# Readouts beside a recurrence: a new order on POOL, ACT and DVE, the last sum folded into ACT, and no ballast products in six bodies

## The chip, the cores and the metric
One core of a Trainium2 chip. The metric is the device time of one execution in microseconds; the time given for a kernel is the median of its runs.

## The reference, cut to what matters
Input x is (8, 512, 64, 2), output (8, 512, 128). Three layers follow each other: a token layer `h` (four small attentions), a recurrent layer whose output is added to h, and a last layer that adds the layernorm of h to h (what else it adds is addressed to channels from 128 on, of which there are none).

```
x_norm = ln(layernorm(h)) ;  xin = x_norm @ W_in.T
res_step: new = tanh(xin_t + prev @ W_res.T);  new = 0.95 * new + 0.05 * prev      # 512 steps
ssm_step: s = A_bar_t * prev + B_bar_t                                             # 512 steps
readout(s) = gelu(ln(s) @ W_ro.T + b_ro)
gate = sigmoid(layernorm(h) @ W_gate.T + b_gate)
h = h + readout(res) * gate + readout(ssm) * (1 - gate)
out = h + layernorm(h)                                                             # rstd*h - rstd*mean + h
```

## The kernel before
Work is cut into 32 tiles, each one batch row and a quarter (128 positions) of the sequence: h_all and gate_all hold them as [128 positions, tile, 128 channels]. The recurrence has 512 steps in 32 bodies of 16. All engines run programs written out in one order, coupled by semaphores alone; an instruction that waits holds all behind it on its engine. The order is written by hand: each engine loops over bodies i and steps t, does its part of the step first (`scan`), and then what is placed beside that step.

A step goes round three engines. PE adds W_res times the state to a PSUM region in four groups of small products (L1150 with y16 as high and low weights, L1157, L1150 with y_lo, L1162). ACT reads that with three operations: tanh to fp16 (L535, y16), tanh to fp32 (L536, ys), the carry (L538, kp16). DVE makes the rests y_lo (L838: ys - y16, both in SBUF) and kp_lo (L841). PE needs y_lo and kp_lo before the step is done.

Bodies 0 to 23 have the attention tiles beside the steps, 24 and 25 the set-up of the second recurrence (ssm). In the last six, 26 to 31, three things stand beside the steps:
- `feed(s, c)`, 8 per body (at even t): PE multiplies B (L1284); DVE first runs the ssm scan of the feed before (`recur`, L953, increments ssm_done), then waits for PE's product and makes the next scan's input (L944). PE's feed s waits for ssm_done of the scan s-2: its PSUM bank is then free.
- `sigma`, DVE scans that turn the tanh values into states (L889): a full row of 128 at t = 1 and 5, and in bodies 28 to 31 a half row of 64 at t = 3, 7, 11, 15.
- `readout(u, n, ...)`, with u = t % 4 and n the group number: every group of four steps starts one readout tile, and five tiles are under way at once. In group n the functions work on tiles n (reads), n-1 (statistics, r_dev, L1005), n-2 (gelu, blend), n-3 (layernorm statistics, norm) and n-4 (last sum).

A tile's way through the readout: PE reads (L1299, four products: (0,0) in u=1, (0,1) in u=2, (1,0) in u=3, (1,1) in the next u=0; ballast products of 512 columns, `keep_clock`, L1074, ahead of the first and third). DVE takes statistics of both reads (L991, L998). POOL makes r_var and r_dev (L454, L458). DVE scales the reads out of PSUM (L1005, readout_scaled). ACT does gelu (L581). POOL blends: difference, base, product, sum into h_all (L436, L437, L465, L471). DVE takes the statistics for the layernorm (L982, L987). POOL makes -mean, var + eps, rstd and -mean*rstd (L443 to L449, ln_small). ACT scales and shifts h_all into gate_all (L574, `norm`), POOL adds h_all to that (L429), and SP's queue writes the tile out on r_out (L350). ACT also halves and shifts the gate (L593).

Reads of tile n go to two PSUM banks that tile n-2 had. PE therefore waits, ahead of the first read:

```
pe.wait_ge(readout_scaled, n - (3 if alone else 1) + TWO_FREE)      # TWO_FREE: counts that are there from the start
```

After the last step `rest_of_readouts` runs the remaining 12 groups with nothing beside them (`alone=True`); there DVE does the blend (L961 to L969).

## Time and profile before

| | |
|---|---|
| time, median of 3 runs | 720.89 us (720.78 to 721.06) |
| the profiled execution: its time, its span | 724.85 us, 723.1 us |
| busy: PE, DVE, ACT, POOL | 654.3 (90%), 567.7 (79%), 424.3 (59%), 193.9 (27%) us |
| last chain by engine | PE 65%, DVE 14%, POOL 9%, issue 7%, ACT 4% |
| POOL busy, tenths, last 10 of 40 slices | 3 8 7 8 7 8 7 7 7 6 |
| granted PE clock, the same slices | 9 9 9 9 9 9 9 9 9 7 |

The shares are of the whole span; the change touches the last 164 us, from about 559 us on, where POOL is busy for 7 to 8 tenths. A clock digit of 9 stands for 90% of full speed or more. The recurrence ends at 680.5 us, the 12 groups without steps after that.

### The profile page before, as it was taken

Reading aid. Unit: us, or ns where it says so; the run is one execution under the profiler, and the core shown is the slowest. Engines: PE = TensorE matmul, PEld = TensorE weight load, DVE = VectorE, ACT = ScalarE, POOL = GpSimd, SP = SyncE. Lnnn points to the kernel's source line nnn. Section 1 sums busy time; section 2 is a strip of 40 time slices with the busy share of each in tenths; the row PEclk is TensorE's granted clock in tenths of the full one; section 3 lists DMA queues with packets and bytes.
Section 4 is the critical chain, followed back from the end, with each engine's and each line's share of the span. In section 5 each row is a group of like instructions: output and inputs, shape, how many; then the busy total and the mean of one; then the engine's idle time right before and its main releaser. Section 6 shows DMA issues by size and latency. Waiting matters only on the chain.

```text
span 723.1 us, 28488 instructions
## 1 busy us (share of the span) xinstructions
PE 654.3 (90%) x11161; PEld 500.4 (69%) x11161; DVE 567.7 (79%) x2438; ACT 424.3 (59%) x2051; POOL 193.9 (27%) x429
## 2 busy tenths in 40 slices
PE   6777777789999999999999999999999999999772
PEld 2334444447888888888888888888787777777641
DVE  4685454567888888989899899899647788988885
ACT  3455544447766776677767776677464444444432
POOL 1133333331000100000000000000000387878776
PEclk9677788899999999999999999999999999999997
DMA  5000000000000000000000000000000000000000
GB/s 185 1 0 1 2 1 1 1 2 3 4 3 4 4 3 5 3 3 4 3 4 3 4 3 4 4 3 5 2 3 2 2 17 14 13 18 13 13 19 26
DMA packets 6326, 7.27 MB, mean 10 GB/s; under 512 B 688, under 2 KB 4784, under 8 KB 6192
## 3 DMA queue, kind: packets, MB, share of 16 engines
q1 hardware_dynamic: 5904, 4.46, 2.0%
q8 instruction: 88, 1.44, 0.9%
q10 hardware_dynamic: 288, 0.99, 0.4%
q14 instruction: 46, 0.38, 0.2%
HBM read 3.35 MB, written 2.10 MB: 8 GB/s over the span
## 4 chain that ended last, share of the span: by engine, by line
PE 65%; DVE 14%; POOL 9%; issue 7%; ACT 4%; DMA 1%; POOLq 0%; DVEq 0%; ACTq 0%
PE PS L1150 22%; PE PS L1202 13%; PE PS L1074 4%; PE PS L1162 4%; PE PS L1117 3%; PE PS L1168 2%; PE PS L1118 2%; POOL r_dev L458 2%; PE PS L1127 2%; PE PS L1051 2%; POOL ln_small L446 2%; PE PS L1104 2%; PE PS L1087 2%; PE PS L1157 2%; DVE top L761 1%
## 5 line engine op out<-in xcount | busy, mean ns | idle before, releaser
L535 ACT ACTIVATE y<-PS 128x16 f16<-128x16 f32 x512 | 94.3, 184 | 167.9 <-PE PS L1162 165.6
L1202 PE MATMUL PS<-ballast,ident 128*128 128x220 f16 (+5 forms) x722 | 150.9, 284 | 0.0
L1150 PE MATMUL PS<-y_lo,res_hi 128*128 128x8 f16 x2048 | 128.7, 169 | 8.8 <-DVE y_lo L838 7.2
L838 DVE TENSOR_TENSOR y_lo<-ys,y 128x16 f16<-128x16 f32 x512 | 95.4, 186 | 51.3 <-ACT ys L536 47.3
L1150 PEld LDWEIGHTS PS<-y,res_hi 128*128 128x128 f16 x2048 | 96.6, 96 | 55.6 <-ACT y L535 21.4
L1150 PE MATMUL PS<-y,res_hi 128*128 128x8 f16 x2048 | 128.8, 169 | 0.4 <-ACT y L535 0.3
L1150 PE MATMUL PS<-y,res_lo 128*128 128x8 f16 x2048 | 123.4, 166 | 0.0
L841 DVE SCALAR_TENSOR_TENSOR kp_lo<-PS,setup,kp 128x16 f16<-128x16 f32 x512 | 114.8, 224 | 0.0
L401 POOL TENSOR_TENSOR small<-small,minus_half 128x2 f32<-128x2 f32 x32 | 22.7, 709 | 340.9 <-DVE y_lo L838 280.1
L517 ACT ACTIVATE prob<-PS,exp_up,sc 128x512 f32<-128x512 f32 x128 | 101.0, 789 | 17.8 <-PE PS L1104 17.8
L761 DVE TENSOR_REDUCE top<-PS 128x1 f32<-128x512 f32 x128 | 86.8, 681 | 21.4 <-PE PS L1087 21.4
L1074 PE MATMUL PS<-ballast,ident 128*128 128x512 f16 (+1 forms) x275 | 89.2, 401 | 15.6 <-DVE ys L889 9.6
L522 ACT ACTIVATE prob_hi<-PS,exp_up,sc 128x512 f16<-128x512 f32 x128 | 100.8, 788 | 0.0
L536 ACT ACTIVATE ys<-PS 128x16 f32<-128x16 f32 x512 | 99.0, 193 | 0.0
L1150 PEld LDWEIGHTS PS<-y_lo,res_hi 128*128 128x128 f16 x2048 | 85.4, 96 | 18.1 <-DVE y_lo L838 13.2
L538 ACT ACTIVATE kp<-PS 128x16 f16<-128x16 f32 x512 | 97.3, 190 | 0.0
L1162 PE MATMUL PS<-kp_lo,carry_id 128*128 128x16 f16 x512 | 92.2, 180 | 0.0
L1150 PEld LDWEIGHTS PS<-y,res_lo 128*128 128x128 f16 x2048 | 87.5, 96 | 0.0
L1157 PE MATMUL PS<-kp,carry_id 128*128 128x16 f16 x512 | 86.5, 169 | 0.0
L791 DVE TENSOR_TENSOR prob_lo<-prob,prob_hi 128x512 f16<-128x512 f32 x96 | 65.4, 682 | 0.0
L1117 PE MATMUL PS<-keep,prob_hi 128*128 128x66 f16 x512 | 51.0, 198 | 6.3 <-ACT prob_hi L522 6.2
L1202 PEld LDWEIGHTS PS<-ballast,ident 128*128 128x128 f16 x722 | 56.5, 97 | 0.2
(205 smaller groups left out, 1337.7 us busy)
## 6 DMA issues: line engine op xcount, KB each, us to landing
ys<-in_x SPq DMA_DIRECT2D x8, 256.0 KB, 7.5
out<-gate_all SPq DMA_DIRECT2D x32, 64.0 KB, 1.5
mats<-in_mats ACTq DMA_DIRECT2D x1, 709.0 KB, 5.3
rows<-in_rows ACTq DMA_DIRECT2D x1, 257.5 KB, 7.5
wall<-in_wall SPq DMA_DIRECT2D x1, 256.0 KB, 5.0
```

The source lines that it names most:

```text
L517: a_.activation(prob[:, a, :], X[a], ACT.Exp, scale=e_col[:, j % B:j % B + 1], bias=exp_up[:, :])
L522: a_.activation(prob_hi[:, a, :], X[a], ACT.Exp, scale=e_col[:, j % B:j % B + 1], bias=exp_up[:, :]).then_inc(prob_ready, 1)
L535: a_.activation(y16[:, :].rearrange("p (m b) -> p m b", m=NH), pre, ACT.Tanh, scale=back).then_inc(y16_ready, 1)
L536: a_.activation(ys[:, :, bass.ds(i * STEPS + (1 + t), 1)].rearrange("p (m b) o -> p m (b o)", m=NH), pre, ACT.Tanh, scale=back).then_inc(a ...
L538: a_.activation(kp16[:, :].rearrange("p (m b) -> p m b", m=NH), pre, ACT.Copy, scale=keep_scale).then_inc(kp_ready, 1)
L838: v.tensor_tensor(y_lo[:, :], ys[:, :, bass.ds(i * STEPS + (1 + t), 1)].rearrange("p n o -> p (n o)"), y16[:, :], ALU.subtract).then_inc(l ...
L841: v.scalar_tensor_tensor(kp_lo[:, :].rearrange("p (m b) -> p m b", m=NH), PRE[t % 2][:, r, :, t // 2, :], setup[:, 24:25], kp16[:, :].rear ...
L1074: t_.matmul(bank[:, 0:size], ident16[:, :], ballast[:, 0:size], start=True, stop=True, skip_group_check=True)
L1150: t_.matmul(dst[:, m, :], wts[:, k, m * P:m * P + P], st[:, k * B:k * B + B], start=False, stop=False, skip_group_check=True)
L1157: t_.matmul(dst, carry_id[:, :], kp16[:, :].rearrange("p (m b) -> p m b", m=NH), start=False, stop=False, skip_group_check=True)
L1162: t_.matmul(dst, carry_id[:, :], kp_lo[:, :].rearrange("p (m b) -> p m b", m=NH), start=False, stop=True, skip_group_check=True).then_inc( ...
L1202: t_.matmul(at[:, 0:size], ident16[:, :], ballast[:, 0:size], start=False, stop=True, skip_group_check=True)
```

## The change
On POOL, in the groups beside steps: the layernorm's small operations (now a function `last_norm`, for tile n-4) move from u=2 to u=0, the four blend operations stand together in u=2, and r_var/r_dev move from u=2 to u=3. The sum L429 is gone: `last_norm` adds one operation, rstd + 1, and ACT's norm computes (1 + rstd) * h - mean * rstd in one pass and releases the output itself. On ACT, gelu moves from u=0 to u=1, and norm, still in u=3, works on tile n-4. On DVE, the scaling of the reads (now `scale_reads`) moves from u=3 to the next u=0, the layernorm statistics from u=0 and 1 to u=1 and 2, the half scans from u=3 to u=0, and the feeds, on PE too, from u = 0 and 2 to u = 2 and 3. The ballast products ahead of reads remain only in the groups without steps. PE's waits are unchanged.

```diff
@@ POOL @@
             def readout(u, n, e, active, fed, kept_bodies, alone=False):
-                if 4 in active and u == (3 if alone else 0):
-                    j = n - 4
-                    pool.wait_ge(readout_normed, j + 1 + TWO_FREE)
-                    pool.sem_inc(pool_waited, 1)
-                    res = gate_all[:, bass.ds(j, 1), :].rearrange("p o n -> p (o n)")
-                    g.tensor_tensor(res, res, h_all[:, bass.ds(j, 1), :].rearrange("p o n -> p (o n)"), ALU.add
-                                    ).then_inc(r_out, 1)
-                if 2 in active and u == 1 and not alone:
+                def last_norm(j, s):
+                    pool.wait_ge(ln_stats, j + 1 + FREE)
+                    if j > 1:
+                        pool.wait_ge(r_out, j - 1)
+                    g.tensor_tensor(ln_small[:, s, 2:3], ln_mv[:, s, 0:1], minus_one[:, :], ALU.mult)
+                    g.tensor_tensor(ln_small[:, s, 0:1], ln_mv[:, s, 1:2], eps_col[:, :], ALU.add).then_inc(ln_var_ready, 1)
+                    pool.wait_ge(ln_var_ready, j + 1)
+                    g.tensor_tensor(ln_small[:, s, 1:2], ln_small[:, s, 0:1], minus_half[:, :], ALU.pow
+                                    ).then_inc(ln_pow_ready, 1)
+                    pool.wait_ge(ln_pow_ready, j + 1)
+                    g.tensor_tensor(ln_small[:, s, 0:1], ln_small[:, s, 1:2], ones[:, 0:1], ALU.add)
+                    g.tensor_tensor(ln_small[:, s, 2:3], ln_small[:, s, 2:3], ln_small[:, s, 1:2], ALU.mult
+                                    ).then_inc(ln_dev_ready, 1)
+
+                if 4 in active and u == 0 and n <= IN_SCAN:
+                    last_norm(n - 4, e)
+                if 2 in active and u == 2 and not alone:
                     j = n - 2
                     now = h_all[:, bass.ds(j, 1), :].rearrange("p o n -> p (o n)")
                     pool.wait_ge(r_gelu, j + 1 + TWO_FREE)
                     pool.wait_ge(h2_ready, j + TWO_FREE)
                     g.tensor_tensor(r_diff, r_act[:, e, 0, :], r_act[:, e, 1, :], ALU.subtract).then_inc(r_diff_ready, 1)
                     g.tensor_tensor(r_base, r_act[:, e, 1, :], now, ALU.add).then_inc(r_base_ready, 1)
-                if 3 in active and u == (3 if alone else 2):
-                    j = n - 3
-                    s = 1 - e
-                    pool.wait_ge(ln_stats, j + 1 + FREE)
-                    pool.wait_ge(readout_normed, j - 1 + TWO_FREE)
-                    g.tensor_tensor(ln_small[:, s, 2:3], ln_mv[:, s, 0:1], minus_one[:, :], ALU.mult)
-                    g.tensor_tensor(ln_small[:, s, 0:1], ln_mv[:, s, 1:2], eps_col[:, :], ALU.add).then_inc(ln_var_ready, 1)
-                    pool.wait_ge(ln_var_ready, j + 1)
-                    g.tensor_tensor(ln_small[:, s, 1:2], ln_small[:, s, 0:1], minus_half[:, :], ALU.pow
-                                    ).then_inc(ln_pow_ready, 1)
-                    pool.wait_ge(ln_pow_ready, j + 1)
-                    g.tensor_tensor(ln_small[:, s, 2:3], ln_small[:, s, 2:3], ln_small[:, s, 1:2], ALU.mult
-                                    ).then_inc(ln_dev_ready, 1)
-                if 1 in active and u == 2:
-                    ...
+                if 1 in active and u == (2 if alone else 3):
+                    j = n - 1
+                    pool.wait_ge(r_stats, j + 1)
+                    g.tensor_tensor(r_var[:, :], r_mv[:, :, 1:2].rearrange("p r o -> p (r o)"), r_eps[:, :], ALU.add
+                                    ).then_inc(r_var_ready, 1)
+                    pool.wait_ge(r_var_ready, j + 1)
+                    pool.wait_ge(readout_scaled, j - 1 + TWO_FREE)
+                    g.tensor_tensor(r_dev[:, 1 - e, :], r_var[:, :], minus_half[:, :].to_broadcast([P, 2]), ALU.pow
+                                    ).then_inc(r_dev_ready, 1)
+                if 3 in active and u == 3 and alone:
+                    last_norm(n - 3, 1 - e)
@@ ACT @@
-                                  scale=ln_small[:, s, 1:2], bias=ln_small[:, s, 2:3]).then_inc(readout_normed, 1)
+                                  scale=ln_small[:, s, 0:1], bias=ln_small[:, s, 2:3]).then_inc(r_out, 1)
-                if 2 in active and u == 0 and not alone:
+                if 2 in active and u == 1:
                     gelu(n - 2)
-                if 2 in active and u == 1 and alone:
-                    gelu(n - 2)
-                if 3 in active and u == 3 and not alone:
-                    norm(n - 3, 1 - e)
-                if 4 in active and u == 2 and alone and n > IN_SCAN:
+                if 4 in active and u == (2 if alone else 3):
                     norm(n - 4, e)
@@ DVE @@
-                if i >= BODIES - NQ and t in (3, 7, 11, 15):
+                if i >= BODIES - NQ and t % 4 == 0:
                     n = (i - (BODIES - NQ)) * 4 + t // 4
                     sigma_row(n % NH, NT - B + n // NH, 0, P // 2, sigma_half)
+            def scale_reads(j, e):
+                dve.wait_ge(r_dev_ready, j + 1 + FREE)
+                dve.wait_ge(r_gelu, j - 1 + TWO_FREE)
+                for r in range(2):
+                    last = v.scalar_tensor_tensor(r_pre[:, e, r, :], PS[:, read_banks(j, e) + r, H:H + P],
+                                                  r_dev[:, e, r:r + 1], ro_row[:, :], ALU.mult, ALU.add)
+                last.then_inc(readout_scaled, 1)
...
-                if 3 in active and u == (2 if alone else 0):
+                if 3 in active and u == (2 if alone else 1):
...
-                if 3 in active and u == (2 if alone else 1):
+                if 3 in active and u == 2:
...
-                if 1 in active and u == 3:
-                    ...
+                if 1 in active and u == 3 and alone:
+                    scale_reads(n - 1, 1 - e)
+                if 2 in active and u == 0 and n <= IN_SCAN:
+                    scale_reads(n - 2, e)
...
-                    if t % 2 == 0:
-                        feed(t // 2, i - FIRST_DECAY)
+                    if t % 4 > 1:
+                        feed(t // 4 * 2 + t % 2, i - FIRST_DECAY)
                     body_readouts(readout, t, i)
@@ PE @@
                         pe.wait_ge(readout_scaled, n - (3 if alone else 1) + TWO_FREE)
-                    keep_clock(PS[:, read_banks(n, e), :])
+                    if alone:
+                        keep_clock(PS[:, read_banks(n, e), :])
                     read_one(0, 0, n, e)
                 if 0 in active and u == 2:
                     read_one(0, 1, n, e)
                 if 0 in active and u == 3:
                     pe.wait_ge(ssm_done, fed + EIGHT_FREE)
-                    keep_clock(PS[:, read_banks(n, e) + 1, :])
+                    if alone:
+                        keep_clock(PS[:, read_banks(n, e) + 1, :])
                     read_one(1, 0, n, e)
...
-                    if t % 2 == 0:
-                        feed(t // 2, i - FIRST_DECAY)
+                    if t % 4 > 1:
+                        feed(t // 4 * 2 + t % 2, i - FIRST_DECAY)
                     body_readouts(readout, t, i)
```

## Rows read from the trace of the kernel before

**Rows 1.** L535 in bodies 27 and 28 to 31: count, min/median/max ns, first and last start.
```profile
L535 ACT ACTIVATE y<-PS x16: 184/184/185, 577.1 to 597.0; 128x16 f16<-128x16 f32 x16
...
L535 ACT ACTIVATE y<-PS x64: 184/184/185, 598.5 to 680.5; 128x16 f16<-128x16 f32 x64
```

**Rows 2.** Timeline, one group with a full scan: start, us, engine, line, out<-in [idle before].
```profile
603.42 0.47 PE L1284 MATMUL PS<-xn,b_t 128*128 128x128 f32 x2
603.60 0.18 ACT L535 ACTIVATE y<-PS 128x16 f16<-128x16 f32 x1 [0.28 <-PE PS L1162]
...
604.14 0.61 DVE L1005 SCALAR_TENSOR_TENSOR k<-PS,r_dev,ro_row 128x128 f32<-128x128 f32 x2 [0.62 <-POOL r_dev L458]
604.16 0.24 PE L1150 MATMUL PS<-y,res_hi 128*128 128x8 f16 x4
...
604.79 0.42 ACT L581 ACTIVATE k<-k 128x256 f32<-128x256 f32 x1 [0.85 <-DVE k L1005]
...
605.69 0.45 POOL L436 TENSOR_TENSOR k<-k 128x128 f32<-128x128 f32 x1
...
605.78 0.39 DVE L838 TENSOR_TENSOR y_lo<-ys,y 128x16 f16<-128x16 f32 x1
...
606.24 0.59 DVE L889 TENSOR_TENSOR_SCAN ys<-keep_row,ys 128x128 f32<-128x128 f32 x1
...
606.59 0.18 ACT L535 ACTIVATE y<-PS 128x16 f16<-128x16 f32 x1 [1.00 <-PE PS L1162]
...
607.48 0.16 DVE L838 TENSOR_TENSOR y_lo<-ys,y 128x16 f16<-128x16 f32 x1
...
607.70 0.47 DVE L953 TENSOR_TENSOR_SCAN keep<-keep 128x128 f32<-128x128 f32 x1
...
608.05 0.18 ACT L535 ACTIVATE y<-PS 128x16 f16<-128x16 f32 x1 [0.83 <-PE PS L1162]
...
608.43 0.14 DVE L838 TENSOR_TENSOR y_lo<-ys,y 128x16 f16<-128x16 f32 x1
...
608.51 0.24 PE L1150 MATMUL PS<-y,res_hi 128*128 128x8 f16 x4
...
608.63 0.34 DVE L889 TENSOR_TENSOR_SCAN ys<-keep_row,ys 128x64 f32<-128x64 f32 x1
...
609.05 0.18 ACT L535 ACTIVATE y<-PS 128x16 f16<-128x16 f32 x1 [0.29 <-PE PS L1162]
```

**Rows 3.** Timeline, the group before: y_lo and POOL starting together.
```profile
600.37 0.45 POOL L437 TENSOR_TENSOR k<-k,h_all 128x128 f32<-128x128 f32 x1
600.37 0.48 DVE L838 TENSOR_TENSOR y_lo<-ys,y 128x16 f16<-128x16 f32 x1 [0.24 <-ACT ys L536]
```

**Rows 4.** Timeline of POOL, a group without a full scan, from r_dev to r_dev.
```profile
634.63 0.70 POOL L458 TENSOR_TENSOR r_dev<-r_var,minus_half 128x2 f32<-128x2 f32 x1
...
635.96 0.46 POOL L471 TENSOR_TENSOR h_all<-k 128x128 f32<-128x128 f32 x1 [0.20 <-POOL k L465]
636.38 0.57 POOL L429 TENSOR_TENSOR gate_all<-gate_all,h_all 128x128 f32<-128x128 f32 x1
636.91 0.45 POOL L436 TENSOR_TENSOR k<-k 128x128 f32<-128x128 f32 x1
...
637.73 0.19 POOL L443 TENSOR_TENSOR ln_small<-ln_mv,minus_one 128x1 f32<-128x1 f32 x1
...
639.59 0.70 POOL L458 TENSOR_TENSOR r_dev<-r_var,minus_half 128x2 f32<-128x2 f32 x1
```

**Rows 5.** Timeline, the end of the kernel: POOL on the last two tiles.
```profile
717.42 0.19 POOL L449 TENSOR_TENSOR ln_small<-ln_small 128x1 f32<-128x1 f32 x1
...
718.73 0.19 POOL L443 TENSOR_TENSOR ln_small<-ln_mv,minus_one 128x1 f32<-128x1 f32 x1
...
720.67 0.45 POOL L429 TENSOR_TENSOR gate_all<-gate_all,h_all 128x128 f32<-128x128 f32 x1 [0.70 <-ACT gate_all L574]
```

**Rows 6.** Busy time by engine in a stretch; after POOL the granted clock, DMA share, GB/s.
```profile
510.00:514.00 4.00, 4.00 (x81) 3.13 (x79) 1.47 (x10) 1.29 (x12) 0.00 (x0) 0.58 0.02 4
```

More of the change, by code:

```diff
@@ L284, in build @@
         ln_dev_ready = sem("ln_dev_ready")
-        readout_normed = sem("readout_normed")
         stats_waited = sem("stats_waited")
@@ L293, in build @@
         start_free = (r_dev_ready, ln_stats)
-        start_two_free = (ln_dev_ready, readout_normed, readout_scaled, r_gelu, h2_ready)
+        start_two_free = (ln_dev_ready, readout_scaled, r_gelu, h2_ready)
         def tile_q(j):
@@ L999, in readout @@
                     last.then_inc(r_stats, 1)
-                if 1 in active and u == 3:
-                    j = n - 1
-                    dve.wait_ge(r_dev_ready, j + 1 + FREE)
-                    dve.wait_ge(r_gelu, j - 1 + TWO_FREE)
-                    for r in range(2):
-                        last = v.scalar_tensor_tensor(r_pre[:, 1 - e, r, :], PS[:, read_banks(n - 1, 1 - e) + r, H:H + P],
-                                                      r_dev[:, 1 - e, r:r + 1], ro_row[:, :], ALU.mult, ALU.add)
-                    last.then_inc(readout_scaled, 1)
+                if 1 in active and u == 3 and alone:
+                    scale_reads(n - 1, 1 - e)
+                if 2 in active and u == 0 and n <= IN_SCAN:
+                    scale_reads(n - 2, e)
             dve.wait_ge(pv_done, NA * NT)
```

8 lines of the change are left out of this document (removed).

## The prediction

> **What bounds the kernel now.** First I read the starts of L535, the tanh with which every step of the recurrence begins on ACT, body by body: body 27 has its first and last start at 577.1 and 597.0, bodies 28 to 31 (64 steps) run from 598.5 to 680.5 [rows 1]. With the step after each, body 27 takes 21.4 us (577.1 to 598.5) and each of the last four about 20.8 (82.0 x 64/63 / 4), 5.2 per group of four steps (u = 0 to 3), in which one readout tile goes through.
>
> Then the timeline of one group of body 28 [rows 2]. The reader is to see two things. A step that is not held up takes 1.00 (608.05 to 609.05). The others are: the group takes 5.45. In u=0 DVE's L1005 waits 0.62 for POOL's r_dev, and the step's y_lo stands behind it; in u=1 y_lo (L838) takes 0.39 instead of 0.14, because POOL's L436 is reading SBUF (605.69 to 606.14); in u=2 it is late behind a full-width scan and the statistics (606.24 to 607.48). Third, POOL's own queue in a group without a full scan [rows 4]: from r_dev to r_dev 4.96, There POOL is the bound, as far as these rows follow each other without a gap (L471, L429, L436); where a full scan is due (t=1 and 5, half of the groups), DVE's queue adds to it. PE is never the one that is late for long.
>
> **What goes.** (a) L429, POOL's last sum: 0.53 to the next start (636.38 to 636.91) [rows 4], against one more 128x1 operation at 0.14 (its neighbours are 0.19 long and overlap). POOL's queue then takes 4.96 - 0.53 + 0.14 = 4.57, or less where it waits for DVE within that: a bound of at most 4.6. (b) The readout chain is spread out: r_dev is computed in u=3, used by L1005 in the next u=0, gelu in u=1, the blend on POOL in u=2. The 0.62 stall of y_lo goes. (c) 48 ballast products (2 in each of 24 groups). In u=3 a step with ballast and a read still took 1.00, so that one was hidden; in u=1 DVE was late anyway. I cost them at 0; if nothing had hidden them, at their own length, under 0.4 each, 18 us in all would be the other end, which the 1.00 step excludes.
>
> **What is late next.** I walk through a group of bodies 28 to 31, with y0 = 0 the start of its first tanh, from [rows 2, 3]. y_lo comes at +0.38 (608.43 - 608.05), other DVE work starts at +0.58 (608.63). That is now the half scan, 0.34 long, some 0.26 to the next start, since DVE's operations overlap by 0.08 (estimate); then L1005, 0.61, done at 1.45. Two waits that stand unchanged in the code now bite, because what they wait for was moved:
>
> (d) PE's first read of the tile in u=1 waits for readout_scaled of the tile two before, whose banks it takes. That was done in the last group before; now it is L1005 in this very group. PE has to stand with the read at the head of its queue, and the next step's matmuls behind it, until 1.49. From a read's start to the next tanh it is 0.43 + 0.54 = 0.97: feed and read hold the next step's matmuls back by 0.74 (603.42 to 604.16), of which I give the feed 0.31 and the read 0.43 by their columns (estimate), and from those matmuls to the tanh it is 0.54 (608.51 to 609.05). So y2 = 2.46. Without (d) it would be 2.0; now it is 2.99 (603.60 to 606.59), so the first two steps still win 0.5.
>
> (e) PE's feed in u=3 waits for ssm_done of the feed two before, which DVE makes in the feed just before it. These were two steps apart; in u=2 and u=3 they are one apart. DVE's scan L953 is 0.47 long [rows 2] and starts 0.58 after y2, so PE can feed at y2 + 1.10. With 0.74 and 0.54 behind it y4 = y2 + 2.38, where steps of 1.09 and 1.00 pass in groups without a full scan. This loses 0.2.
>
> (f) The four 128x128 operations of POOL, 0.45 each, now stand in u=2. gelu (0.42) starts after L1005 at 1.49, so POOL begins at 1.98, the product at 2.80, the sum at 3.46 (two in 0.82, and [0.20] of waiting before the sum, [rows 4]). y_lo of u=2 comes at 2.46 + 0.38 = 2.84: it meets the product. [Rows 3] show what that costs: L838, started together with L437, ended when that did, 0.48 against 0.14. So y_lo is some 0.4 late, and with it L953, PE's feed and y4: 2.46 + 2.38 + 0.4 = 5.2. If it slips in ahead of the product, 4.85. With a full scan, DVE reaches y_lo at 1.58 + 0.4 + 0.2 + 0.65 = 2.85 by itself (1.24 from 606.24 to 607.48 is a slowed scan plus the 0.65 of L991), the same place, so 5.2 as well. Full-scan groups take 5.4 now, the others 5.0.
>
> In [rows 2] L838 that came during L436 ended within 0.03 of its end, while the scan L889, which met L437 for 0.3, took 0.59, only 0.12 more than L953, a scan of the same size. The Trainium skill, page "SBUF — State Buffer", section "Who interferes with whom", says that a DVE instruction with two SBUF inputs and a GpSimd instruction that reads SBUF share one interface, and that whichever starts first blocks the other entirely. The row of L838 agrees, that of the scan only in part. By that rule the moved blend speaks against the change: y_lo loses up to 0.45 in u=2, and the group is 5.2 to 5.3; by the scan's row it would be 4.95.
>
> **The sum.** Bodies 28 to 31: 16 groups; 8 with a full scan save 0.2 each (5.4 to 5.2), 8 without lose 0 to 0.2; together -0.5, with ends -6 (4.85 in all groups) and +5 (5.5). Body 27 has no half scan: L1005 is done at 1.19, y2 = 2.20, gelu starts at 1.34 behind ACT's own three operations; y_lo at 2.58 comes while POOL's second operation runs (2.24 to 2.69), 0.15 lost; its groups take 4.6 and, with a full scan, 5.0: 19.2, so -2.2 (ends -4 and 0). Body 26: its first two groups, without a readout to wait for, lose 0.2 each by (e), the other two win that; 0. The end of the kernel [rows 5]: the last norm on POOL started at 718.73 behind the sum of the tile before; now it can at 717.42 + 0.14 + 0.20 = 717.76, and ends 0.14 later; the last sum after the last norm, 0.70 waited and 0.45 long, of which 0.50 is the ACT operation itself, goes with 0.65: -0.97 + 0.14 - 0.65 = -1.5. The first tile after the recurrence: reads start once DVE is through its queue, which has the same operations in another order; -0.3 (ends -0.5 and +0.3). Other tiles of this stage are bound by DVE's unchanged queue: 0. Sum: -0.5 - 2.2 - 1.5 - 0.3 = -4.5, on the profiled execution 724.85 to 720.3. The median of the runs, 720.89, lies 3.96 below that execution, and I take the same difference: 716.4.
>
> **The rivals.**
> 1. The clash with POOL is missed: y_lo gets in ahead of the product, groups of 4.6 to 4.85. For it: the margin is a few hundredths, in [rows 2] y_lo got in at the end of L436 although L437 was due, and POOL may shift. Against it: [rows 3]. 16 groups x 0.35 to 0.6 = 5.6 to 9.6 instead of 0.5: 707 to 711.5, say 710.
> 2. Nothing is left but the end: the last four bodies come out a little longer than now, as the two waits on PE and the port give back more than was won; the time is 720.
> 3. Slower: wait (e) compounds with (f). y_lo of u=2 loses 0.45, the scan L953 behind it meets POOL's sum and takes 0.12 more, and y_lo of u=3 meets that sum too, 0.15. The group is then 2.46 + 2.38 + 0.45 + 0.12 + 0.15 = 5.55, 16 x 0.35 = 5.6 lost, 4.0 won elsewhere, of which 1 goes in body 27: 723.5. It decides from a group of 5.2 + 4.0/16 = 5.45. For it: all these operations are back to back in u=2 and u=3. Against it: the sum ends at 3.92, and y_lo of u=3 isn't due before 4.1.
> 4. The clock falls without ballast. The granted clock was 0.58 from 510 to 514 though PE was busy the whole of it [rows 6], so a busy PE is no guarantee. Against it: reads and feeds stay, and the group is no longer. At the half clock PE's reads and feeds, about 2.2 of a group, double: from 2 or 3 such groups on the gain is gone, over the whole stage it would be 40 us.
>
> **How the numbers follow.** Forecast 0.43 (716.4; 713.5 to 719); rival 1 0.25; rival 2 0.16; rival 3 0.12; rival 4 0.04. About 0.2% (1.4 us) can be told from no change: faster 0.43 + 0.25 + 0.06 of rival 2 = 0.74; within 0.2% the other 0.10 of rival 2 and 0.01 of rival 3 = 0.11; slower 0.11 + 0.04 = 0.15. The range 708.5 to 722.5 leaves out the far part of rival 1, the top of rival 3 and rival 4.
>
> **What would show it.** L1005 without a wait for r_dev in the scan stage; the tanh to tanh time of u=1 at 1.3 to 1.5 with PE waiting for L1005; PE's feed in u=3 waiting for L953; L838 of u=2 at 0.4 or more beside POOL's L465; in the last lines no POOL operation after the last norm. It is wrong if POOL's r_dev still ends the wait of u=0, if the half scan isn't what delays the read in u=1 (bodies 26 and 27 should be faster than the later ones), or if the granted clock shows dips between 560 and 680.

## The result and the profile after

The kernel got slower. Its median is 737.28 us (729.05 to 738.45, 4 runs) against 720.91 us for the kernel before, run beside it: a ratio of 1.0196, 95% interval 1.0147 to 1.0244. The prediction was 716.4 (708.5 to 722.5). The profiled execution took 737.34 us with a span of 735.5 us; before it was 724.85 and 723.1. In the later sets three single executions of the kernel before, at 746.46, 747.73 and 923.14 us, lie far off all the others and are left out of the ratios.

The page of after, first the busy times by engine, then the granted PE clock in tenths over 40 slices of 18.4 us:

```profile
PE 666.2 (91%) x11113; PEld 508.2 (69%) x11113; DVE 565.1 (77%) x2438; ACT 422.9 (57%) x2051; POOL 188.6 (26%) x429
...
PEclk9788888899999999999999999999996557599998
```

PE has 48 products fewer (11113 against 11161) and is busy 11.9 us longer. The weight loads beside it (PEld) grew too, 508.2 against 500.4; DVE, ACT and POOL did not. The clock line says why: where the line of before has 9, five slices from about 552 us on have 6, 5, 5, 7, 5. They lie in the stretch from which the ballast was taken out; the last slices of that stretch are back at 9.

The busy times by stretch (stretch in us; its length; busy us and instructions of PE, PEld, DVE, ACT, POOL; granted clock as a share of 2.4 GHz; DMA share; GB/s) show it closer:

```profile
556.00:560.00 4.00, 3.27 (x50) 2.82 (x51) 2.15 (x12) 1.81 (x13) 0.00 (x0) 0.88 0.01 2
560.00:602.00 42.00, 42.00 (x441) 32.49 (x440) 26.21 (x124) 12.74 (x89) 20.13 (x52) 0.50 0.02 6
602.00:608.00 6.00, 6.00 (x68) 5.12 (x65) 3.38 (x16) 2.21 (x15) 4.12 (x11) 0.60 0.04 11
608.00:614.00 6.00, 5.50 (x87) 4.45 (x85) 5.22 (x26) 2.40 (x17) 3.62 (x9) 1.00 0.05 14
614.00:620.00 6.00, 5.18 (x64) 4.10 (x65) 4.83 (x24) 2.42 (x15) 4.62 (x14) 0.75 0.05 14
620.00:641.00 21.00, 20.54 (x217) 15.95 (x214) 13.88 (x66) 6.92 (x45) 12.00 (x33) 0.50 0.04 11
641.00:695.00 54.00, 45.64 (x724) 37.73 (x721) 46.48 (x224) 25.64 (x161) 42.37 (x114) 1.00 0.05 15
```

For 42 us from 560 on the clock is at 0.50, the lower of its two levels (1.2 GHz), with PE busy for all 42.00 of them. It is back between 608 and 614, lost again until 641, and then stays at 1.00 to the end of the recurrence. PE runs 10.5 products per us in the second row and 13.4 in the last. So within this kernel a high busy share of PE is the sign of the low clock: each product lasts longer. One line's products, the reads out of `keep` between 577 and 602 and between 650 and 694 (median and longest in ns stand in the middle and at the end of the three numbers), last longer at the low clock:

```profile
L1295 PE MATMUL PS<-ro_pair,keep x16: 634/634/774, 579.7 to 601.2; 128*128 128x256 f32 x16
L1295 PE MATMUL PS<-ro_pair,keep x34: 379/380/463, 650.1 to 691.3; 128*128 128x256 f32 x34
```

The medians are 634 and 380 ns: x1.67, not 2, for half the clock.

A group at the low clock, in order of time (start, duration, engine, line and operation, in brackets the idle time before it and what ended it). L531 is the tanh with which a step begins, L1280 the feed, L1295 the read:

```profile
590.40 0.78 PE L1280 MATMUL PS<-xn,b_t 128*128 128x128 f32 x2
590.58 0.18 ACT L531 ACTIVATE y<-PS 128x16 f16<-128x16 f32 x1 [0.83 <-PE PS L1158]
...
590.96 1.06 PE L1295 MATMUL PS<-ro_pair,ys 128*128 128x256 f32 x2
...
592.42 0.18 ACT L531 ACTIVATE y<-PS 128x16 f16<-128x16 f32 x1 [1.22 <-PE PS L1158]
...
594.26 0.18 ACT L531 ACTIVATE y<-PS 128x16 f16<-128x16 f32 x1 [1.13 <-PE PS L1158]
...
595.67 0.18 ACT L531 ACTIVATE y<-PS 128x16 f16<-128x16 f32 x1 [1.08 <-PE PS L1158]
```

No PE line has a wait in brackets: PE goes from product to product, and everything else waits for it. Steps with feed and read take 1.84 (590.58 to 592.42 to 594.26), the one with a read alone 1.41 (594.26 to 595.67); with the fourth step, 1.47, the group is 6.6.

The same at the full clock, bodies later:

```profile
675.80 0.18 ACT L531 ACTIVATE y<-PS 128x16 f16<-128x16 f32 x1 [0.73 <-PE PS L1158]
676.61 0.58 DVE L967 SCALAR_TENSOR_TENSOR k<-PS,r_dev,ro_row 128x128 f32<-128x128 f32 x2
676.71 0.18 ACT L531 ACTIVATE y<-PS 128x16 f16<-128x16 f32 x1 [0.57 <-PE PS L1158]
...
677.34 0.67 PE L1295 MATMUL PS<-ro_pair,ys 128*128 128x256 f32 x2 [0.66 <-DVE k L967]
...
678.38 0.18 ACT L531 ACTIVATE y<-PS 128x16 f16<-128x16 f32 x1 [0.74 <-PE PS L1158]
678.55 0.46 POOL L451 TENSOR_TENSOR k<-k,gate_all 128x128 f32<-128x128 f32 x1
678.69 0.35 DVE L830 TENSOR_TENSOR y_lo<-ys,y 128x16 f16<-128x16 f32 x1
679.10 0.47 DVE L945 TENSOR_TENSOR_SCAN keep<-keep 128x128 f32<-128x128 f32 x1
679.47 0.18 ACT L531 ACTIVATE y<-PS 128x16 f16<-128x16 f32 x1 [0.47 <-PE PS L1158]
679.62 0.49 PE L1280 MATMUL PS<-xn,b_t 128*128 128x128 f32 x2 [0.18 <-DVE keep L945]
...
680.92 0.18 ACT L531 ACTIVATE y<-PS 128x16 f16<-128x16 f32 x1 [0.73 <-PE PS L1158]
```

Steps 0.91, 1.67, 1.09, 1.45: the group is 5.12 where it was 5.45 [rows 2]. So the change does what it is for, once the clock is there. L967, which answers to L1005, waits for nothing; the waits that the prediction called (d) and (e) are both there in brackets, 0.66 and 0.18.

Body by body, from first tanh to first tanh, bodies 26 to 31 (the last without its last step):

```
before  17.97  21.38  20.58  20.80  20.81  19.81    sum 121.35
after   24.64  26.63  24.72  22.87  20.45  19.02    sum 138.33
```

The sum grows by 17.0 us. What follows the last tanh takes 1.9 less (735.5 - 694.8 = 40.7 against 723.1 - 680.5 = 42.6), and this execution reached body 26 2.7 us earlier, before any changed instruction (its early stretch had no dip such as [rows 6] has). 17.0 - 1.9 - 2.7 = 12.4, the difference of the spans. Without the 2.7, which the change did not bring, it is 15.1, near the 16.4 of the medians.

Where the clock first fell, at about 559: the last thing ahead of it is a load of ACT's function table at the end of body 25, and with it the widest stop of PE thereabouts.

```profile
555.19 1.28 ACT L599 ACT_TABLE_LOAD   x1
...
556.73 0.26 PE L1146 MATMUL PS<-y,res_hi 128*128 128x8 f16 x4 [0.83 <-ACT y L531]
```

The kernel before has the same load (557.88, 1.28 us) and keeps its clock; there a feed stands in the stop, and PE waits 0.32 instead of 0.83.

Where it rose, at about 607 and 641, PE was running the input products of the step regions (L1164), a short stretch of extra work, or had just done so:

```profile
605.36 1.20 PE L1164 MATMUL PS<-xd,in_t 128*128 128x128 f32 x4
...
639.10 0.77 PE L1164 MATMUL PS<-xd,in_t 128*128 128x128 f32 x2
```

### The profile page after: what moved, and what is told of

Its sections match the earlier page's. It is cut to its first block, busy times and chain, and to the rows that moved or that the text cites. A ratio compares the mean times of both kernels' runs of the same rounds, so it can differ in the third digit from the quotient of the medians.

```text
span 735.5 us, 28357 instructions
## 1 busy us (share of the span) xinstructions
PE 666.2 (91%) x11113; PEld 508.2 (69%) x11113; DVE 565.1 (77%) x2438; ACT 422.9 (57%) x2051; POOL 188.6 (26%) x429
## 3 DMA queue, kind: packets, MB, share of 16 engines
q8 instruction: 87, 1.43, 0.8%
## 4 chain that ended last, share of the span: by engine, by line
PE 75%; DVE 14%; issue 5%; ACT 4%; POOL 1%; DMA 1%; DVEq 0%; POOLq 0%; ACTq 0%
PE PS L1146 24%; PE PS L1198 13%; PE PS L1295 7%; PE PS L1070 4%; PE PS L1158 4%; PE PS L1280 3%; PE PS L1164 3%; PE PS L1113 2%; PE PS L1114 2%; PE PS L1123 2%; PE PS L1153 2%; DVE k L967 2%; PE PS L1100 2%; PE PS L1083 2%; PE PS L1047 1%
## 5 line engine op out<-in xcount | busy, mean ns | idle before, releaser
L531 ACT ACTIVATE y<-PS 128x16 f16<-128x16 f32 x512 | 94.3, 184 | 201.0 <-PE PS L1158 199.9
L830 DVE TENSOR_TENSOR y_lo<-ys,y 128x16 f16<-128x16 f32 x512 | 94.3, 184 | 84.4 <-ACT ys L532 79.9
L1146 PEld LDWEIGHTS PS<-y,res_hi 128*128 128x128 f16 x2048 | 100.9, 99 | 65.1 <-ACT y L531 21.8
L1146 PE MATMUL PS<-y,res_hi 128*128 128x8 f16 x2048 | 130.9, 170 | 0.9 <-ACT y L531 0.8
L1070 PE MATMUL PS<-ballast,ident 128*128 128x512 f16 (+1 forms) x227 | 71.2, 406 | 14.7 <-DVE ys L881 8.8
```

Of the source, the lines that this page charges most:

```text
L531: a_.activation(y16[:, :].rearrange("p (m b) -> p m b", m=NH), pre, ACT.Tanh, scale=back).then_inc(y16_ready, 1)
L830: v.tensor_tensor(y_lo[:, :], ys[:, :, bass.ds(i * STEPS + (1 + t), 1)].rearrange("p n o -> p (n o)"), y16[:, :], ALU.subtract).then_inc(l ...
L1070: t_.matmul(bank[:, 0:size], ident16[:, :], ballast[:, 0:size], start=True, stop=True, skip_group_check=True)
L1146: t_.matmul(dst[:, m, :], wts[:, k, m * P:m * P + P], st[:, k * B:k * B + B], start=False, stop=False, skip_group_check=True)
```

## The experiments

The theory after the result: the whole loss is the clock, and the ballast products are what kept it. The rivals: the new order itself is slower (its waits on PE, the clash with POOL), and the low clock is only a mark beside that; or the new order, by its gaps, is what drops the clock, and the ballast has no part. Later runs ask where in the group ballast has to stand, and what the order is worth by itself. All kernels ran with the kernel before beside them; its medians were 723.45, 723.26, 723.98 and 723.31 in the four sets, so ratios are what compares. Each kernel has one traced execution, and what is said of its groups and its clock is of that one.

### Ballast back in the new order

```diff
-                    if alone:
-                        keep_clock(PS[:, read_banks(n, e), :])
+                    keep_clock(PS[:, read_banks(n, e), :])
...
-                    if alone:
-                        keep_clock(PS[:, read_banks(n, e) + 1, :])
+                    keep_clock(PS[:, read_banks(n, e) + 1, :])
```

> The kernel after with the two ballast products of each group back in the six bodies, and nothing else. Theory A (the granted clock is the loss: the kernel after ran about 12 groups of its six bodies at the half clock, 6.57 a group against 5.12 at the full one): the clock stays at 1.00 from 560 to the end of the recurrence. The ballast isn't free in the new order, since PE is what is late there: 0.22 more in u=1, behind the wait for L1005, and 0.22 in u=3, behind the wait for the feed, so groups of 5.5 and a time near 724, between before (720.9) and after (737.3). Theory B (the waits that the new order puts on PE let the clock fall, with ballast or without): half clock in these bodies again, 733 or more.

Measured: 724.01 (722.04 to 726.54, 10 runs), 1.0017 [0.9998, 1.0035]. By stretch:

```profile
555.00:568.00 13.00, 12.05 (x173) 9.63 (x172) 8.01 (x37) 4.88 (x32) 0.00 (x0) 0.87 0.02 4
568.00:685.00 117.00, 103.80 (x1572) 86.00 (x1570) 95.14 (x468) 51.62 (x329) 87.51 (x232) 1.00 0.05 13
```

The clock falls at the same place, about 560, but comes back after some 3.4 us (0.87 over 13 us), and then holds 1.00 for 117 us. That gives back nearly all of the loss: 1.96% slower becomes no difference that can be told. The order is not what makes it slow. But it is not faster than before either: groups take 5.32 (0.91, 1.81, 1.09, 1.52) and not 5.12, 0.14 of it in u=1 and 0.07 in u=3, because in u=1 the ballast now starts only when PE's wait for L967 is over, ahead of the read, on the path:

```profile
650.01 0.58 DVE L967 SCALAR_TENSOR_TENSOR k<-PS,r_dev,ro_row 128x128 f32<-128x128 f32 x2
...
650.74 0.38 PE L1070 MATMUL PS<-ballast,ident 128*128 128x512 f16 x1 [0.67 <-DVE k L967]
...
650.96 0.59 PE L1295 MATMUL PS<-ro_pair,ys 128*128 128x256 f32 x2
```

PE stood idle 0.67, and then did ballast: 0.22 from its start to the read's.

### The old order without ballast

The kernel before, with the two `if alone:` of the change and nothing else of it.

```diff
-                    keep_clock(PS[:, read_banks(n, e), :])
+                    if alone:
+                        keep_clock(PS[:, read_banks(n, e), :])
```

> The kernel before without the ballast products of the reads beside steps, its order unchanged. Theory A (ballast holds the clock in any order): the granted clock falls in these bodies and the time is 728 or more. Theory B (it is the new order that lets it fall): the clock holds as before, groups stay at 4.96 and 5.45, 720 to 721.

Measured: 748.1 (747.19 to 750.22, 4 runs), 1.0344 [1.0325, 1.0364]. By stretch:

```profile
560.00:602.00 42.00, 42.00 (x443) 32.48 (x443) 27.60 (x125) 13.29 (x94) 20.20 (x52) 0.50 0.02 7
602.00:644.00 42.00, 41.33 (x440) 32.87 (x440) 31.50 (x138) 14.90 (x96) 26.86 (x71) 0.58 0.05 13
644.00:686.00 42.00, 39.95 (x489) 31.80 (x488) 33.69 (x151) 16.67 (x105) 29.57 (x77) 0.70 0.05 13
686.00:708.00 22.00, 22.00 (x235) 17.24 (x233) 17.06 (x73) 7.91 (x53) 14.33 (x39) 0.50 0.04 10
```

The second rival falls: the old order loses the clock in the same place, and stays without it longer. Removing the ballast costs 25 us in the old order (748.1 - 723.45) and 13 in the new one (737.28 - 724.01, over two sets). In the traces the old order was low for longer, since it lost the clock three times (at about 560, 618 and 669) and the new one twice; one execution of each doesn't show that the order is the reason.

### Ballast in the first body only

```diff
-                    if alone:
+                    if alone or n < 4:
```

> The kernel after with ballast in body 26 alone (the first four groups), where the clock fell. Theory A1 (the sparse first groups are what lets it fall, later ones hold a full clock): 1.00 throughout, groups of 5.12, 714 to 717. Theory A2 (the groups without ballast can't hold it in general; it fell a second time at 614 to 620 in the run of after): half clock somewhere in bodies 27 to 31, 725 or more.

Measured: 723.9, 727.19, 735.42 and 728.75, median 727.97, 1.0104 [1.0048, 1.0161]. The profiled one is the fastest, and its clock row

```profile
568.00:681.00 113.00, 97.67 (x1535) 81.03 (x1534) 96.42 (x467) 52.02 (x331) 86.67 (x232) 1.00 0.05 13
```

shows 113 us at 1.00 with no ballast in five of the six bodies, and PE busy for 86% only. Theory A1 is wrong in its first part, since the clock fell at 561 even with this ballast and was back at 568. At the full clock the groups without ballast can hold it. But the other three executions took 3 to 12 us more, as theory A2 has it, and where they lost it is not known, since they have no trace.

### Ballast in the first three steps of body 26 only

```diff
+                    if i == FIRST_READ and t < 3:
+                        for _ in range(3):
+                            keep_clock(PS[:, 3, :])
```

> The kernel after with nine ballast products in the first three steps of body 26 and none later. There PE stood idle behind ACT's table load and the clock fell. Theory C (the loss is one fall at a sparse place, from which groups without ballast don't come back): with the place filled the clock stays at 1.00 in most executions, 717 to 720. Theory D (the groups without ballast let it fall by themselves): falls further on, 725 or more in most executions, a wide spread.

Measured: 726.23 (723.71 to 733.04, 10 runs), 1.0050 [1.0023, 1.0076].

```profile
560.00:577.00 17.00, 15.76 (x242) 12.77 (x239) 12.25 (x59) 6.26 (x47) 5.24 (x11) 1.00 0.01 2
577.00:608.00 31.00, 29.77 (x356) 23.98 (x355) 21.45 (x104) 11.26 (x74) 19.86 (x54) 0.67 0.04 10
```

With nine products beside the first steps the fall at 560 is gone from the trace. The profiled execution, the slowest of the ten (span 731.3), then lost the clock at about 585, in body 27, had it back at 606 behind the input products, and lost it again from 619 to 636. So the fall at 560 is not the only one: without ballast it can fall at other places. That is theory D: 7 of the 10 executions took over 725 us, and none came to the 717 to 720 of theory C. Against the change with its clock kept (0.9960, below) the median is 0.9% longer, where it was 2.4% without any ballast, so more than half of the loss goes with the fall at 560.

### Feeds apart again, with ballast

```diff
-                    if t % 4 > 1:
-                        feed(t // 4 * 2 + t % 2, i - FIRST_DECAY)
+                    if t % 2 == 0:
+                        feed(t // 2, i - FIRST_DECAY)
```

> The kernel after with ballast back and with the feeds at u=0 and 2 again (and one more wait of DVE on its own count ahead of the first row after the recurrence, which its order needs). Theory (the wait of PE's feed on the scan of the feed just before is worth 0.2 to 0.3 a group): against the kernel after with ballast alone, u=3 shrinks from about 1.66 to 1.0, but L1005 comes a feed (0.57) later in u=0 and with it the read in u=1, so groups of 5.3 to 5.5, 0 to 3 us faster than it, 721 to 724. Rival (feeds' place does not matter, the port clash of y_lo does): the same time within 1 us.

The two ballast products are back here, and DVE has the one more wait that the expectation names.

Measured: 723.66 (720.91 to 725.34, 10 runs), 1.0007 [0.9992, 1.0022]; groups 5.38 (1.09, 2.20, 1.09, 1.00). The wait (e) is gone, u=3 falls from 1.52 to 1.00, and what it gave is paid in u=0 (1.09 for 0.91, it has a feed now) and u=1 (2.20 for 1.81): DVE's scan L945 and L936 now stand ahead of L967, which ends later, and the ballast and the read wait for it. Undoing this part neither gains nor loses.

### Half scan behind the scaling, with ballast

```diff
-                if i >= BODIES - NQ and t % 4 == 0:
...
+                    half_sigma(t, i)                   # the same scan, behind body_readouts
```

> The kernel after with ballast back, and the half scan of bodies 28 to 31 behind the scaling of the reads (L967) in u=0 instead of ahead of it. Theory (PE's first read of a tile waits for L967, which the half scan holds up by 0.26): u=1 shrinks from 1.81 to 1.57 as in body 27, groups from 5.32 to 5.1, 3 to 4 us less than with ballast back alone (724.0), near 720.5. Rival (DVE's whole queue is the bound, so its order doesn't matter): the same time, and the 0.26 shows up in u=1 or u=2 again.

Measured: 723.4 (719.55 to 725.12, 10 runs), 1.0007 [0.9988, 1.0026]. In the trace u=1 falls from 1.81 to 1.57 and the groups from 5.32 to 5.22 and 5.08, so the half scan does delay L967, as (d) has it; 16 groups by 0.1 to 0.24 are 1.6 to 3.8 us, and less than the runs scatter. What (d) says is shown by the trace; that it is worth time is not shown by the times.

### Ballast where PE waits anyway

```diff
                 if 0 in active and u == 1:
+                    if not alone:
+                        pe.wait_ge(ssm_scaled, ...)
+                        for _ in range(1):
+                            keep_clock(PS[:, 7, :])
...
+                    if t % 4 == 3:
+                        keep_clock(PS[:, read_banks(0, t // 4 % 2) + 1, :])
```

> The kernel after with the same two ballast products a group, but where PE stands idle: in u=1 ahead of the wait for L967 (into a feed bank that is free by then), in u=3 ahead of the feed's wait (into the bank of the next read). Theory (the kernel after lost by the clock alone, and its waits leave room for ballast): groups of 5.12 at the full clock, no half clock from body 27 on, about 4 us less than with ballast back in its old places: 718 to 720, faster than before by 3 to 5. Rival (ballast costs its length wherever it is, or does not hold the clock there): 723 or more.

Measured: 720.99 (718.26 to 722.64, 10 runs), 0.9965 [0.9949, 0.9981]. The product in u=1 stands now ahead of the wait for L967, in bank 7, a feed's bank that is free by then, the other ahead of the feed's wait in u=3. Groups are 5.12 and, in body 27, 4.92, as with no ballast, at

```profile
568.00:679.00 111.00, 104.19 (x1555) 80.08 (x1553) 95.09 (x459) 51.29 (x324) 86.60 (x232) 1.00 0.05 14
```

Against the first experiment the stretch of the six bodies is 4.9 us shorter in the traces (120.6 against 125.5, 24 groups by 0.2), and what follows the last tanh 1.1 longer (40.8 against 39.7), perhaps because DVE is further behind by then, which was not looked into. That leaves 3.8 us, and the ratios, 1.0017 and 0.9965, say 3.8 as well.

### One ballast product a group

The same with the product in u=1 alone.

> The kernel after with one ballast product a group, in u=1 ahead of the wait for L967, none in u=3. Theory (what lets the clock fall is how little PE streams in a group, in degrees): between the kernel after (737) and the one with two idle products (721.0), in an execution either held or not: 721 to 730, with a wide spread of its runs. Rival (only the idle stretch ahead of L967 matters, not the amount): as with two, 721.

Measured: 720.83 (719.91 to 721.93, 7 runs), 0.9960 [0.9948, 0.9972]; groups 5.12.

```profile
568.00:677.00 109.00, 98.40 (x1501) 77.98 (x1498) 93.79 (x454) 50.85 (x321) 85.42 (x229) 1.00 0.05 14
```

One product of 0.38 us in a group, beside a wait, makes the difference between 737.28 (1.0196) and 720.83 (0.9960), 2.4%. The theory of degrees gets no support: the time is that of two products, as the rival has it, and the runs lie close together. This is the nearest to what the prediction had in mind: the change in full, at the full clock but for 559 to 562.5.

### Ballast in the gaps and the half scan last

> Ballast in the idle places, two products in u=1, and the half scan behind L967. Both theories together: groups of 4.9 in bodies 27 to 31, full clock, 714 to 717. If the second ballast product in u=1 no longer fits ahead of L967 (0.4 of idle for 0.43 of products), 0.1 more a group.

Measured: 717.39 (715.72 to 719.31, 4 runs), 0.9922 [0.9891, 0.9952], groups 5.01 and 4.87. (It has two products in u=1 and one in u=3.) Against the kernel with one product in each place (720.99, same set) it is 3.6 us faster. In the traces 2.4 of that lie in bodies 28 to 31 (78.2 against 80.6), where the half scan's place tells, and 1.2 in body 26 (18.86 against 20.08), which here kept its clock at 560. So the half scan's place, which hid in the scatter above, is worth some 2.4 us.

### The folded sum alone

The kernel before, with nothing of the change but `last_norm`'s extra operation and ACT's one pass instead of POOL's L429.

```diff
                     g.tensor_tensor(ln_small[:, s, 0:1], ln_small[:, s, 1:2], ones[:, 0:1], ALU.add)
...
-                                  scale=ln_small[:, s, 1:2], bias=ln_small[:, s, 2:3]).then_inc(readout_normed, 1)
+                                  scale=ln_small[:, s, 0:1], bias=ln_small[:, s, 2:3]).then_inc(r_out, 1)
```

> The kernel before, its order, its ballast, with the last sum folded into ACT's norm and nothing else. Theory (POOL's queue is the bound of the groups without a full scan, and the end is a chain over POOL): groups of 4.96 become 4.6, those of 5.45 stay as they are (their POOL waits for DVE), and the end is 1.5 shorter: 3 to 5 us less than before. Rival (DVE's and PE's queue take over at once): only the 1.5 of the end.

Measured: 717.23 (716.91 to 719.3, 4 runs), 0.9930 [0.9904, 0.9956]. POOL from r_dev to r_dev:

```profile
670.18 0.70 POOL L452 TENSOR_TENSOR r_dev<-r_var,minus_half 128x2 f32<-128x2 f32 x1
...
674.92 0.70 POOL L452 TENSOR_TENSOR r_dev<-r_var,minus_half 128x2 f32<-128x2 f32 x1
```

4.74 where [rows 4] have 4.96. This one part, with order and ballast left as they were, brings 0.70%; in the traces it is 4.5 us in the six bodies (116.9 against 121.35) and 1.5 behind them (41.0). Most groups run at 4.75 to 5.15. Nothing else of the change is needed for it.

### Feeds in u=1 and u=3, half scan last, ballast in the gaps

```diff
-                    if t % 4 > 1:
-                        feed(t // 4 * 2 + t % 2, i - FIRST_DECAY)
+                    if t % 2 == 1:
+                        feed(t // 2, i - FIRST_DECAY)
...
-                if 3 in active and u == (2 if alone else 1):     # layernorm statistics, one step later
+                if 3 in active and u == 2:
...
                 if 0 in active and u == 1:
+                    if not alone:
+                        pe.wait_ge(ssm_scaled, ...)
+                        keep_clock(PS[:, 7, :])
...
                 if 0 in active and u == 2:
+                    if not alone:
+                        keep_clock(PS[:, read_banks(n, e) + 1, :])
```

> The new order with PE's feeds at u=1 and 3, so that the first stands in PE's idle time ahead of the read that waits for L967 and no feed follows the one before it directly; half scan behind L967; layernorm statistics of DVE one step later; ballast in u=1 behind the feed and in u=2. Theory (the two waits (d) and (e) are all that holds the new order's groups at 5.1): u=3 falls from 1.45 to 1.1, u=1 stays 1.4, u=2 grows to 1.2 to 1.4 since DVE then has the scan of the feed in u=1; groups of 4.7, with a full scan 5.0 to 5.1: 714 to 717, level with the half scan moved and ballast idle (717.4) or a little better. Rival (DVE's queue in u=1, with full scan, feed and statistics 1.9, takes over entirely): groups of 5.1 to 5.3, 719 to 722.

Measured: 715.3 (715.13 to 716.42, 4 runs), 0.9880 [0.9863, 0.9897], the fastest of all, better than both kernels. From the timeline (L1283 is the feed here, L1073 the ballast, L1298 the read, L1161 the step's last product):

```profile
647.34 0.47 PE L1283 MATMUL PS<-xn,b_t 128*128 128x128 f32 x2
647.52 0.18 ACT L531 ACTIVATE y<-PS 128x16 f16<-128x16 f32 x1 [0.58 <-PE PS L1161]
...
647.64 0.38 PE L1073 MATMUL PS<-ballast,ident 128*128 128x512 f16 x1
...
647.91 0.67 PE L1298 MATMUL PS<-ro_pair,ys 128*128 128x256 f32 x2
...
648.95 0.18 ACT L531 ACTIVATE y<-PS 128x16 f16<-128x16 f32 x1 [0.74 <-PE PS L1161]
```

The feed and the ballast now fill PE's time ahead of the read of u=1, and u=1 takes 1.43 (647.52 to 648.95) with a feed in it, against 1.67 without one. Feeds two steps apart wait for nothing; what PE still waits for, in a group with a full scan, is y_lo (L830), some 0.3 each time. Groups without a full scan take 4.64, the others 5.0.

### The same without its ballast

> The fastest order so far (feeds at u=1 and 3, half scan behind L967; 715.3 with two ballast products a group) without those products. Theory (groups without ballast don't get the clock back once it has fallen at the start of body 26, in any order): half clock for long stretches, 725 or more. Rival (an order that packs PE's work into shorter groups needs no ballast): 713 to 716, at most one short fall.

Measured: 731.4 (730.57 to 733.17, 4 runs), 1.0123 [1.009, 1.0156].

```profile
560.00:608.00 48.00, 48.00 (x509) 37.25 (x510) 29.95 (x144) 14.96 (x106) 21.49 (x57) 0.51 0.02 6
608.00:688.00 80.00, 73.39 (x1115) 60.29 (x1113) 71.76 (x342) 37.49 (x240) 64.26 (x176) 0.97 0.06 16
```

The fall at about 561 again, and the return at about 612, behind the input products (608.2 to 611.7), as in the kernel after; the 0.97 of the second row is its first 4 us. From there it holds the clock to the end of the recurrence, with groups of 4.64 and 5.0. So the theory is right about the time and wrong that such groups never get the clock back. With ballast this kernel gains 16 us. In the three orders without ballast (after, the old one, this one) the first fall is at the same place, and how much is lost further on differs.

## Why the prediction was wrong

The step that failed is (c), the ballast, costed at 0, and with it the chance of 0.04 for rival 4. The mechanism of rival 4 is what happened. The prediction asked what the 48 products take, and its bound from the other side was their length. What it had to ask is what they give: the trace of before held no stretch of these bodies without them, so its 1.00 step could not exclude anything. The argument against rival 4, "reads and feeds stay, and the group is no longer", was an argument without a row; [rows 6] spoke for the rival: a clock of 0.58 with PE busy throughout. The rival's size was on the high side: it let PE's 2.2 us a group double, and a group at the low clock took 6.56 against 4.92 in body 27 and 6.80 against 5.12 later, 1.6 and 1.7 more. "From 2 or 3 such groups on the gain is gone" holds, at just under three.

What the clock took can be added up from bodies of the new order that ran at the full clock. Body 26 took 24.64 against 18.86 (ballast in the gaps and the half scan last), bodies 27, 28 and 29 took 26.63, 24.72 and 22.87 against 19.68, 20.68 and 20.47 (ballast in the first body only): 5.8 + 6.9 + 4.0 + 2.4 = 19.2 us, where 20.9 lie between the forecast, 716.4, and the median, 737.28.

Its other steps, read at the full clock:

- The terms of the sum: body 26 +0.9 (18.86 against 17.97) where 0 was given, body 27 -1.7 (19.68) where -2.2 was, bodies 28 to 31 -1.4 (80.6 against 82.0) where -0.5 was, what follows them -1.9 where -1.8 was. Together -4.1 against -4.5: near, and in part by luck, since the errors of the bodies take each other away.
- (a) L429 goes, POOL's queue shortens: right in kind. With the fold alone 4.74 from r_dev to r_dev, 0.22 less where 0.39 was given; whether POOL or the steps set those 4.74 was not taken apart.
- (b) the stall of L1005 goes: right; no wait stands before L967.
- (d) PE's read waits for L967 in u=1: right. PE's read starts 1.54 after the tanh of u=0 (675.80 to 677.34), predicted 1.49; the first two steps take 2.58, predicted 2.46. PE's waits between 654 and 694 (who waits for whom; total us, times, longest):

```profile
PE PS L1295 <- DVE k L967: 5.3, 8, 0.7
PE PS L1280 <- DVE keep L945: 1.5, 8, 0.2
```

- (e) PE's feed in u=3 waits for the scan just before: right in kind; u=2 and u=3 take 2.54, predicted 2.38 with no clash and 2.78 with one. The prediction's "loses 0.2" is a slip: its 2.38 is 0.29 over 1.09 + 1.00.
- (f) y_lo meets POOL's product in u=2: it does, L830 took 0.35 and ended with L451 (679.04 and 679.01). It came out 0.2 longer (0.35 instead of some 0.15) and not 0.4, since L830 started while the product was under way. PE did not wait for it: its products with y_lo began at 679.17, right behind the ones before them, and the step took the 1.09 that the prediction has for such a step. What it can have cost lies in u=3, through the scan L945 behind it (679.10), for which PE's feed waits 0.18. Group: 5.12, predicted 5.2. Rival 1 (groups of 4.6 to 4.85) and rival 3 (5.55) did not occur.
- Body 27, which has no half scan: 4.92 a group where the clock was full (ballast in the first body only), predicted 4.6 and 5.0.
- The tail after the recurrence: 1.9 less, predicted 1.5 + 0.3; with the fold alone it is 1.5 less. It counts from the last tanh, so it also holds what DVE is behind by then: without ballast the old order, which has none of the fold, took 40.7 as well, after slower steps. Its last rows have no POOL operation behind the last norm:

```profile
731.54 0.19 POOL L434 TENSOR_TENSOR ln_small<-ln_small 128x1 f32<-128x1 f32 x1
...
733.09 0.49 ACT L570 ACTIVATE gate_all<-h_all,ln_small 128x128 f32<-128x128 f32 x1 [0.83 <-POOL ln_small L434]
```

With one ballast product beside a wait the change is 0.40% faster (0.9960), where the prediction had 4.5 us, 0.62%. The prediction did not price the fold and the new order apart. The fold alone, in the old order, gives 0.70% [0.9904, 0.9956], against 0.40% [0.9948, 0.9972] for the whole; these are different sets and the intervals overlap a little, and in the traces the two are 6.0 and 3.0 us less than before, about 1 of the difference being the short fall at 560. So nothing shows that the new order as it stands adds to the fold; with its feeds, half scan and ballast moved it does (0.9880).

What stays open is what makes the clock fall, and what brings it back. The granted clock of 560 to 564 in one profiled execution of each kernel:

```
without ballast there:      after 0.50   old order 0.50   feeds in the gap 0.63
with 2 or 1 in a group:     back in the new order 0.68   first body 0.69   half scan last 0.64
                            idle (1 + 1) 0.57   one 0.69   feeds in the gap 0.61
                            before 1.00   fold alone 1.00   feeds apart 1.00
with more:                  half scan last, 3 in a group 1.00   nine in the first steps 1.00
```

Each kernel without ballast fell. Of those with one or two products a group six fell and came back within one or two groups (first body only: at 568), and three held. Those three have PE standing for 0.32 us at the table load, with a feed in the stop, the six for 0.82 or 0.83. But the old order without ballast stood 0.32 too and fell, and three products a group stood 0.83 and held. So both the stop and the ballast go with the fall, neither decides it alone, and each kernel has one trace. The table load was not moved in any run, so its part in this was not tried.

The later falls without ballast, at 617 in the kernel after, 618 and 669 in the old order, 585 and 619 with nine products in the first steps, have no table load and no PE wait above 0.7 us near them, and nothing here explains them. Up to the end of the recurrence, each return without ballast came while the input products ran or within 2 us behind them; but such products also ran in the old order, from 640.35 on, without bringing it back before about 652.

## What to carry to other kernels

Before filler work on TensorE is costed by its length, ask what the clock would be without it, and take the price from rows at the low clock: here it was 13 to 25 us for products that were nearly free. Filler belongs ahead of a wait that PE has anyway, not behind it: the same two products cost 0.2 us a group behind PE's waits and nothing ahead of them. And when a change has parts, run them alone: one part here, the sum folded into an ACT pass, gained at least as much alone (0.9930) as the whole change does with its clock kept (0.9960), and the part thought to be free cost 2%.

## What the runs showed of the hardware

- The same groups ran at either level of the clock, for long stretches. Without ballast they held 1.00 for 113 us in one kernel and were at 0.50 for 42 us in another. Neither is sure to last: in the kernel after the clock came back at about 607, was lost at 617, and was back for good at 641.
- PE's busy share says nothing of how safe the clock is. In the kernel after PE was busy for 42.00 of 42.00 us at 0.50 and for 45.64 of 54 at 1.00; with three ballast products a group it was busy nearly throughout at 1.00:

```profile
565.00:610.00 45.00, 44.96 (x661) 33.95 (x657) 38.59 (x187) 20.05 (x132) 32.95 (x87) 1.00 0.04 11
```

- The Trainium skill, page "TensorE: Matmul & The Clock Gate", section "Part 1: The HAM clock gate (the "warmup" mystery)", describes a clock that falls where PE idles and rises where it is busy. Here no wait of PE near the first fall was above 0.83 us, and a PE that the profile shows busy for 42 us without a break (it models the ends of products) did not bring the clock back; the measurement decides.
- One 512-column product a group, 0.38 us in some 5, went with a clock that came back after its fall (0.69 at 560 to 564, 1.00 from 564 on) and stayed to the end of the recurrence; all 7 executions lie within 2.0 us.
- Kernels with ballast in a few places only scatter: 723.9 to 735.4 with ballast in one body, 723.7 to 733.0 with it in three steps, a width of 9 to 12 us, against 1.3 to 5.6 us in the kernels of the new order where every group had some.
- Of the port that DVE and POOL share: y_lo beside POOL's product took 0.35 and not its 0.14 to 0.18, and ended when that did, as in [rows 3].
